# A graph kernel in which ScalarE casts the parts of the gathered table, loads ahead are spread over tiles, a bias product is in bf16, and the last unit is short

## The reference

```
xn = layernorm(x)
x  = x + gcn(xn, src, dst) + mix(xn)            # 256 -> 64, normalised sum over edges, -> 256; linear attention and MLP
h  = layernorm(x)
w  = softmax(h @ Wr + br)                       # 8 gates for each node
x  = x + sum over 8 experts of w[e] * (relu(bn(relu(bn(h @ W1[e])) @ W2[e])) @ Wo[e] + bo[e])
xn = layernorm(x)
x  = x + gat(xn, edges) + mix2(xn)              # graph attention, 8 heads; linear attention
x  = x + sum over 4 experts of g[e] * (gelu(x @ W1[e] + b1[e]) @ W2[e] + b2[e])
         # g: top-2 gates from a second graph attention with 4 heads x 4 experts, layernorm, softmax
```

## Time and profile before

| | us |
|---|---|
| median of 3 runs | 4652.31 (4649.49 to 4652.64) |
| profiled execution, its own time | 4653.68 |
| its span, first to last instruction | 4652.0 |
| TensorE busy | 3793.3 (82%) |
| GpSimd busy | 2800.2 (60%) |
| VectorE busy | 3181.6 (68%) |
| ScalarE busy | 2251.8 (48%) |

### The profile page before, as it was taken

The page is one execution under the profiler, slowest core; times in us unless marked ns, Lnnn a source line. Parts: engine busy times, 40 slices in busy tenths (PEclk is TensorE's granted clock), DMA queues, the critical chain, the costliest instruction groups (busy, mean ns, idle before and its releaser), DMA issues. The chain is left out here.

```text
span 4652.0 us, 67767 instructions
## 1 busy us (share of the span) xinstructions
PE 3793.3 (82%) x17826; PEld 2401.8 (52%) x17828; DVE 3181.6 (68%) x9935; ACT 2251.8 (48%) x4069; POOL 2800.2 (60%) x2880
## 2 busy tenths in 40 slices
PE   6797989999999999758888888887178887787776
PEld 6644556666666566534444444446144454444444
DVE  7775565454646455678888888886566777777776
ACT  7242223322322333357776765444366666666665
POOL 0174576565756410077777777773777777777774
PEclk9998999999999999888988988995588889988988
DMA  3233121111211100455555555653322222222221
GB/s 98 71 91 108 29 48 40 32 42 30 44 28 39 25 12 0 122 135 140 141 133 133 134 131 147 163 150 80 78 35 40 45 40 40 40 39 39 40 40 27
DMA packets 291562, 331.24 MB, mean 71 GB/s; under 512 B 80094, under 2 KB 245886, under 8 KB 291190
## 3 DMA queue, kind: packets, MB, share of 16 engines
q0 software_dynamic: 105328, 175.77, 18.5%
q1 hardware_dynamic: 185862, 151.14, 11.9%
HBM read 289.47 MB, written 30.77 MB: 69 GB/s over the span
## 5 line engine op out<-in xcount | busy, mean ns | idle before, releaser
L3035 POOL DMA_INDIRECT st_rows<-tabr,router_rsrc x1072 | 1022.8, 954 | 329.9 <-issue 321.5
L2388 POOL DMA_INDIRECT all_XT<-tab,graph_gsrc x880 | 855.1, 972 | 308.6 <-issue 244.7
L1416 POOL DMA_INDIRECT st_rows<-tab,graph_gsrc x748 | 742.0, 992 | 482.9 <-PE st_pe L1439 281.0
L1669 ACT ACTIVATE st_h<-st_ph,st_shift,st_scale 128x448 f32<-128x448 f32 x448 | 324.4, 724 | 753.4 <-PE st_ph L1527 753.3
L2418 PE MATMUL st_po<-all_XT,st_hot 128*128 128x264 f32 x1760 | 567.8, 459 | 37.6 <-DVE gat_sum L2609 36.4
L2609 DVE TENSOR_TENSOR gat_sum<-gat_sum,st_po 128x264 f32 x880 | 376.4, 428 | 145.1 <-DVE gat_sum L2609 98.5
L3080 PE MATMUL st_px<-all_XT,st_w 128*128 128x512 f32 (+1 forms) x832 | 423.2, 658 | 10.8 <-ACT st_hid L3140 10.8
L1756 DVE TENSOR_TENSOR gcn_acc<-gcn_acc,st_pe 128x65 f32 x748 | 166.4, 222 | 379.7 <-PE st_pe L1439 289.4
L2418 PEld LDWEIGHTS st_po<-all_XT,st_hot 128*128 128x128 f32 x1760 | 320.3, 211 | 198.7 <-DVE gat_sum L2609 122.5
L3092 PE MATMUL st_py<-st_w,st_hid 128*128 128x256 f32 x1568 | 420.0, 414 | 0.5 <-ACT st_hid L3140 0.5
L3053 PE MATMUL st_pad<-st_adr,st_hott 128*128 x1072 | 121.9, 183 | 345.6 <-DVE st_zd L3206 330.8
(11 more groups left out here) (507 smaller groups left out, 7221.5 us busy)
## 6 DMA issues: line engine op xcount, KB each, us to landing
st_bc<-drowr SPq DMA_DIRECT2D x268, 128.0 KB
st_bc<-drow SPq DMA_DIRECT2D x220, 128.0 KB
st_rows<-tabr,router_rsrc POOLq DMA_INDIRECT x1072
all_XT<-tab,graph_gsrc POOLq DMA_INDIRECT x880
st_xtb<-xtd SPq DMA_DIRECT2D x98, 128.0 KB
st_rows<-tab,graph_gsrc POOLq DMA_INDIRECT x748
tab<-gat_sum SPq DMA_DIRECT2D x7, 924.0 KB
xtd<-all_XT SPq DMA_DIRECT2D x49, 128.0 KB, 1.7
```

Source lines behind the costliest of these rows:

```text
L1416: g.indirect_dma_start(self.rows[:, b, u, :], None, self.R.tab0, bass.IndirectOffsetOnAxis(self.R.gsrc[:, t:t + 1], 0)).then_inc(self.s_ro ...
L1669: a.activation((self.h1, self.h2)[l][:, fb, h * HALF:(h + 1) * HALF], self.ph[:, m % 3, 0:HALF], ACT.Relu, bias=self.shift[:, l, i:i + 1], ...
L2388: g.indirect_dma_start(self.rows[:, b, u, :], None, self.R.tab1, bass.IndirectOffsetOnAxis(self.R.gsrc[:, t:t + 1], 0)).then_inc(self.s_ro ...
L3035: g.indirect_dma_start(self.rows[:, b, u, :], None, self.R.tabr, bass.IndirectOffsetOnAxis(self.R.rsrc[:, t:t + 1], 0)).then_inc(self.s_ro ...
```

## The change

There are four edits. In Front's end ScalarE does the two casts of each chunk, VectorE keeps the scaling and two subtractions, and a loop has three chunks under way: scaled(i), the first subtraction of i-1, the second of i-2. The wait for a free store buffer goes with the first cast to ScalarE.

In Prelude the load of registers moves ahead of the first tile, and the loads ahead are issued one behind each tile's load from tile 3 on. There are 24 of them, since `bo` is now loaded twelve times, into 96 partitions.

In Stage 1 the gates are split into three bf16 parts by seven more small instructions of VectorE in each chunk, and laid out over 96 rows, so that one bf16 product of 96 rows holds all products of parts that are kept. `bo` is split once, at the start of the stage.

In Stage 3 the units are eleven of four windows, one of three and one of two, each judged by itself. An update waits only for the last update of the same window.

```
-        self.bo = f.sb("bo", [E0, D])
+        self.bo = f.sb("bo", [PARTS * 32, D])
+        self.bop = f.sb("bop", [PARTS * 32, D], BF16)
...
+        _, ws = self.nc.values_load_multi_w_load_instructions(
+            self.R.gperm[0:1, 0:TPI], engines=(ENG.SP,), min_val=0, max_val=W - 1,
+            skip_runtime_bounds_check_because="a number of a window")
         for n in range(W):
...
-            if n == W // 2:
-                for to, of in loads:
-                    s.dma_start(to, of).then_inc(self.s_ahead, 16)
-                _, ws = self.nc.values_load_multi_w_load_instructions(
-                    self.R.gperm[0:1, 0:TPI], engines=(ENG.SP,), min_val=0, max_val=W - 1,
-                    skip_runtime_bounds_check_because="a number of a window")
-                for j in range(TPI):
-                    s.dma_start(self.R.ahead.xm[:, :, j * P:(j + 1) * P],
-                                self.R.xtd[bass.ds(ws[j], 1), :, :].rearrange("a p (c t) -> p (a c) t", c=C))\
-                        .then_inc(self.s_ahead, 16)
+            k = n - self.XTB
+            if 0 <= k < len(loads):
+                s.dma_start(*loads[k]).then_inc(self.s_ahead, 16)
+            elif 0 <= k - len(loads) < TPI:
+                j = k - len(loads)
+                s.dma_start(self.R.ahead.xm[:, :, j * P:(j + 1) * P],
+                            self.R.xtd[bass.ds(ws[j], 1), :, :].rearrange("a p (c t) -> p (a c) t", c=C))\
+                    .then_inc(self.s_ahead, 16)
...
+        def cast(i, k):
+            if 0 <= i < ITER:
+                x = self.xw[:, TPI * i:TPI * (i + 1), :]
+                if k == 0:
+                    a.wait_ge(self.s_scaled, i + 1)
+                    if i >= self.TABS:
+                        a.wait_ge(self.s_out[i % self.TABS], 16 * (i // self.TABS))
+                else:
+                    a.wait_ge(self.s_less, i + 1)
+                a.activation(self.tabt[:, i % self.TABS, :, k * GCOL:k * GCOL + GCN], x, ACT.Copy)\
+                    .then_inc(self.s_cast[k], 1)
+        for i in range(ITER + 1):
+            cast(i, 0)
+            cast(i - 1, 1)
...
-        def rows_cut(i):
...
-        for i in range(ITER):
-            rows_cut(i)
+        for i in range(ITER + 2):
+            scaled(i)
+            cut(i - 1, 0)
+            cut(i - 2, 1)
             put(i + 2)
...
-                mm = t.transpose(self.side[0:E0, (j - 4 * k) * P:(j - 4 * k + 1) * P], self.gate[:, n % 2, j, :],
+                mm = t.transpose(self.side[0:PARTS * 32, (j - 4 * k) * P:(j - 4 * k + 1) * P], self.gs[:, j, :],
...
-                mm = t.matmul(self.side[:, (j - 2 * k) * D:(j - 2 * k + 1) * D], self.gt[:, j, :], self.bo[:, :],
+                mm = t.matmul(self.side[:, (j - 2 * k) * D:(j - 2 * k + 1) * D], self.gt[:, j, :], self.bop[:, :],
...
+            if n:
+                v.wait_ge(self.s_side, self.at["gt", n - 1, 1] + 1)
+            st.then(v.tensor_copy(self.gb[:, :, :], self.gate[:, n % 2]))
+            st.then(v.tensor_copy(g4[:, :, :, 0:E0], every(self.gb[:, :, :])))
+            st.then(v.tensor_tensor(self.lg[:, :, :], self.gate[:, n % 2], self.gb[:, :, :], ALU.subtract))
+            st.then(v.tensor_copy(self.gb[:, :, :], self.lg[:, :, :]))
+            st.then(v.tensor_copy(g4[:, :, :, E0:2 * E0], every(self.gb[:, :, :])))
+            st.then(v.tensor_tensor(self.lg[:, :, :], self.lg[:, :, :], self.gb[:, :, :], ALU.subtract))
+            st.then(v.tensor_copy(g4[:, :, :, 2 * E0:3 * E0], every(self.lg[:, :, :])))
...
+        st.then(v.memset(self.gs[:, :, :], 0.0))
+        st.then(v.tensor_copy(self.bop[:, :], self.bo[:, :]))
+        for k in range(1, PARTS):
+            st.then(v.tensor_tensor(self.bo[:, :], self.bo[:, :], self.bop[:, :], ALU.subtract))
+            for b in range(k, PARTS):
+                st.then(v.tensor_copy(self.bop[32 * b:32 * (b + 1), :], self.bo[32 * b:32 * (b + 1), :]))
...
-        self.units = [(r, min(U, W - r)) for r in range(0, W, U)]
+        self.units = [(r, U) for r in range(0, last, U)] + [(last, W - self.LAST - last), (W - self.LAST, self.LAST)]
-        self.judged = [(r, U) for r in range(0, last, U)] + [(last, W - last)]
+        self.judged = list(self.units)
...
-            if self.moved:
-                v.wait_ge(self.s_x, self.moved)
+            if r in self.touched:
+                v.wait_ge(self.s_x, self.touched[r])
```

More of the change, by code:

```diff
@@ L241, in loads @@
                 (self.bg[:, :], spread(A.gcn_b)), (self.wr[:, :, :], rows(A.f0_wr)), (self.br[:, :], spread(A.f0_br)),
-                (self.bo[:, :], A.f0_bo), (self.bn[:, :, :, :], A.f0_bn))
+                (self.bn[:, :, :, :], A.f0_bn)) + tuple(
+                    (self.bo[E0 * k:E0 * (k + 1), :], A.f0_bo) for k in range(PARTS * 32 // E0))
 class Prelude:
@@ L329, in sync @@
         A = self.A
+        loads = self.R.ahead.loads(A)
+        assert self.XTB + len(loads) + TPI <= W
+        _, ws = self.nc.values_load_multi_w_load_instructions(
+            self.R.gperm[0:1, 0:TPI], engines=(ENG.SP,), min_val=0, max_val=W - 1,
+            skip_runtime_bounds_check_because="a number of a window")
         for n in range(W):
@@ L612, in __init__ @@
         self.s_xd = [f.sem(f"xd{j}") for j in range(self.SETS * TPI)]
+        self.s_scaled, self.s_less = f.sem("scaled"), f.sem("less")
+        self.s_cast = [f.sem(f"cast{k}") for k in range(2)]
         (self.s_made, self.s_keyed, self.s_columns, self.s_moved, self.s_ordered, self.s_tabbed, self.s_split, self.s_turned,
@@ L907, in put, with scaled, cut @@
             v.tensor_copy(R.gdst[:, j * P:(j + 1) * P], self.pt[:, j % 2, P:2 * P]).then_inc(self.s_put, 1)
-        def rows_cut(i):
-            part = [self.tabt[:, i % self.TABS, :, k * GCOL:k * GCOL + GCN] for k in range(PARTS)]
-            x = self.xw[:, TPI * i:TPI * (i + 1), :]
-            if i >= self.TABS:
-                v.wait_ge(self.s_out[i % self.TABS], 16 * (i // self.TABS))
-            norm = R.nsrc[:, TPI * i:TPI * (i + 1)].unsqueeze(2).to_broadcast([P, TPI, GCN])
-            st.then(v.tensor_tensor(x, x, norm, ALU.mult))
-            st.then(v.tensor_copy(part[0], x))
-            st.then(v.tensor_tensor(x, x, part[0], ALU.subtract))
-            st.then(v.tensor_copy(part[1], x))
-            v.tensor_tensor(part[2], x, part[1], ALU.subtract).then_inc(self.s_tab, 1)
+        def scaled(i):
+            if i < ITER:
+                x = self.xw[:, TPI * i:TPI * (i + 1), :]
+                norm = R.nsrc[:, TPI * i:TPI * (i + 1)].unsqueeze(2).to_broadcast([P, TPI, GCN])
+                v.tensor_tensor(x, x, norm, ALU.mult).then_inc(self.s_scaled, 1)
+        def cut(i, k):
+            if 0 <= i < ITER:
+                x = self.xw[:, TPI * i:TPI * (i + 1), :]
+                part = [self.tabt[:, i % self.TABS, :, m * GCOL:m * GCOL + GCN] for m in range(PARTS)]
+                v.wait_ge(self.s_cast[k], i + 1)
+                if k == 0:
+                    v.tensor_tensor(x, x, part[0], ALU.subtract).then_inc(self.s_less, 1)
+                else:
+                    v.tensor_tensor(part[2], x, part[1], ALU.subtract).then_inc(self.s_tab, 1)
         v.memset(R.X[:, W - 1, :], 0.0).then_inc(self.s_cleared, 1)
@@ L1307, in __init__ @@
         self.br = R.ahead.br
-        self.bo = R.ahead.bo
+        self.bo, self.bop = R.ahead.bo, R.ahead.bop
+        self.gs = f.sb("gs", [P, TPI, PARTS * 32])
+        self.gb = f.sb("gb", [P, TPI, E0], BF16)
         self.bn = R.ahead.bn
@@ L1329, in __init__ @@
         self.gate = f.sb("gate", [P, 2, TPI, E0])
-        self.gt = f.sb("gt", [E0, TPI, P])
+        self.gt = f.sb("gt", [PARTS * 32, TPI, P], BF16)
         self.h1 = f.sb("h1", [P, C, TOK])
@@ L2884 @@
     UNIT = 4
+    LAST = 2
     START = 23
@@ L2915, in __init__ @@
         U = self.UNIT
-        V = W - (W // U - 1) * U
+        V = U
         self.g20 = f.sb("g20", [P, V, FROW])
@@ L3187, in vector @@
         st = Steps(v, self.s_st)
-        self.moved = 0
+        self.moved, self.touched = 0, {}
         def one_hot(q):
@@ L3424, in finished @@
             s.wait_ge(self.s_x, self.final[u])
-            if r + n < W:
-                ws = self.ranked(ENG.SP, r, n, W - 2)
-                for j in range(n):
-                    s.dma_start(whole[:, bass.ds(ws[j], 1), :], R.X[:, bass.ds(ws[j], 1), :]).then_inc(self.s_out, 16)
-            else:
+            full = min(n, W - 1 - r)
+            ws = self.ranked(ENG.SP, r, full, W - 2)
+            for j in range(full):
+                s.dma_start(whole[:, bass.ds(ws[j], 1), :], R.X[:, bass.ds(ws[j], 1), :]).then_inc(self.s_out, 16)
+            if full < n:
                 s.dma_start(self.out[(W - 1) * P:N, :], R.X[0:N - (W - 1) * P, W - 1, :]).then_inc(self.s_out, 16)
```

9 lines of the change are left out of this document (6 added, 3 removed).

## The result

| | before | changed |
|---|---|---|
| median of 20 runs, us | 4649.08 | 4641.88 |
| ratio | | 0.9982, 95% interval 0.9976 to 0.9988 |
| profiled execution, us | 4653.68 | 4629.89 |

The change is 0.18% faster, about 8 us, where I forecast 27 us and a range of 4615 to 4640: faster, but by a third of it and outside the range. Three single runs far off (4746 and 5008 us of the changed kernel, 4830 us of before) are left out of the ratio. The profiled execution of before, 4653.68 us, lies 4.6 us over its median, and that of the changed kernel is one of the fastest of the changed kernel's runs, which lie between 4628 and 4649 us; before's lie closer, from 4642 to 4656 us. So the two traces show 24 us, and three later traces of nearly the same program have spans that are 15 to 26 us longer. That difference is the first thing to explain.

A forecast was written before the change was run, and what follows sets the result against it. The bound changes with the stage: TensorE in Stage 1, no engine in Stage 3's last loops. Terms -4.1 - 6.7 - 12.4 - 3.8 = -27.0 us from 4653.68 gave 4626.7, so 4626 for the median; range of 8 in 10: 4615 to 4640.

The forecast's parts named there:

- Stage 3: End of Stage 3: shorter last judging and eight updates, less partly covered work moved into the loops, -3.8 us.
- Front, up to the first instruction of the next phase: Front's end: with casts on ScalarE the last subtraction ends at 206.9 instead of 211.01, -4.1 us.
- load of registers at the head of Prelude: Prelude's head: the load, now ahead of the first tile's transfer, is fully on the path, 1.1 us more.
- Prelude's wait and slow tile: Prelude: the burst of loads costs one tile 4.9 + 2.9 = 7.8 us, which spreading the loads saves.
- Stage 1, the product at an equal clock: Stage 1: bf16 bias product saves 0.74 us a pair; of 18.5 us, waits leave -12.4.
- The sum's step to 204.2 us: Front's end: chunk 6's first cast waits for a free store buffer until about 204.2, at 1.4 us per further store.
- My lower end, -1: Front's end: the term's small end, -1 us, if stores take the 6.4 us of the slowest.
- The absorbing waits: Stage 1: TensorE's waits for the third (1.1 us) and fourth (2.5 to 3.0 us) bias additions take back some saving.
- an earlier product only waits longer: Stage 1: L1449 waits for VectorE's third bias addition in six chunks, so a shorter product there gains nothing.
- a rival in Prelude: Prelude: second transfers make 24 tiles late, TensorE runs at its lower level, 70 us lost, 4702 us; chance 0.03.
- the cover in the last loops: Last loops of Stage 3: VectorE's idle time covers 7.2 us of moved judging and updates; last judging begins 4.8 us later.
- Rival 2: End of Stage 3 no faster or slower: moved judging and table loads delay the last loops' products, +3.4, 4633 us; chance 0.2.

The follow-up runs named there:

- e1: The changed kernel once more, as it is, for a second trace: 4643.37 us, ratio 0.9988 to the kernel before.
- e2: The changed kernel with each update again waiting for the update before it: 4645.35 us, ratio 0.9989 to the kernel before.
- e4: The changed kernel with each update waiting for the one before, except in the last unit: 4642.05 us, ratio 0.9986 to the kernel before.
- e14: The kernel of e12 with Front's end as in the kernel before (VectorE casts): 4627.58 us, ratio 0.9958 to the kernel before.
- e13: The kernel before with the new units' products (3 and 2 windows), the last five windows still judged together: 4655.72 us, ratio 1.0021.
- e3: The kernel before with only the updates' waits relaxed: 4653.67 us, ratio 1.0008.
- e12: Changed kernel, Stage 3 as before but last twenty updates free of each other, each chunk's third and fourth bias products done three times: 4626.84 us, 0.9955.
- e16: The kernel of e12, with TensorE also turning the identity 14 times before waiting for the next chunk's rows: 4619.80 us, ratio 0.9944.

## Why the prediction was wrong, by its own steps

The largest miss is Stage 3, 13.1 us between forecast and measured; Front has 4.0 and Stage 1, both rows together, 2.9. The sum with what the traces measured, in us; the last column is the changed kernel's first trace and e1, e2 and e4 in the mean, against the first trace of before (in Stage 1 against the mean of the four with its product). The medians differ by 7.2 us:

| term | forecast | measured |
|---|---|---|
| Front, up to the first instruction of the next phase | -4.1 | -0.1 |
| load of registers at the head of Prelude | +1.1 | +1.2 |
| Prelude's wait and slow tile | -7.8 | -7.9 |
| Stage 1, the product at an equal clock | -12.4 | -17.0 |
| Stage 1, more time at the lower clock | 0 | +7.5 |
| Stage 3 | -3.8 | +9.3 |
| the stretches between | 0 | -1.0 |
| sum | -27.0 | -8.0 |

- **Front.** The step that failed is the end of the term: I took the last subtraction's 4.1 us as the phase's. It came (3.2 us), but the phase ends with the landing of the last store, and I had used landings only for when a buffer comes free. The last store is issued 2.2 to 3.2 us sooner in the four traces, and SP then waits longer for it, 5.3 to 6.4 us where it was 3.1. The sum's step to 204.2 us also has 1.2 us for "the smaller transfer ahead" for which it shows no row. My lower end, -1, was near the value, and e14 shows no more.
- **Registers' load and Prelude**: right in mechanism and size by the traces (first product of a tile to the last: 176.4 us in the mean, before 184.3). No timed run shows it by itself. With the load at its head SP issues the first tile's transfer 1.09 us behind VectorE's first instruction, where it was 0.09 us ahead (216.68 - 215.59, 216.48 - 216.57). The load is a whole 1.2 us on the path, though its first use comes only at tile 27, with the loads of chunk 0; no run has it elsewhere.
- **Stage 1.** The absorbing waits were named rightly, and took 7.2 us. But a pair takes 0.22 us and not 0.31, so that all products together save 7 x (3 x 0.83 + 0.52) = 21.1 us, and TensorE's waits on the edge sums became 2.7 us shorter: 21.1 - 7.2 + 2.7 = 16.6 us. The term at an equal clock was mis-sized by 4.6 us. The step that failed is "an earlier product only waits longer", priced at nothing. A longer wait had a price of its own, the lower clock behind it. The lower clock took back 7.5 us in the mean of these traces, of which a part came behind waits that didn't grow, and that part is unexplained. I had it only as a rival in Prelude, where it didn't come.
- **Stage 3.** The end behind the last judging was right: eight updates in 0.48 + 7 x 0.40 us, the judging even shorter. The step that failed is the cover in the last loops. I priced the moved judging and updates (that cost was 2.3 us), and took the products' plan as unchanged. The split of the products costs 8.2 us (e13), and TensorE's waits between halves that are joined through ScalarE's queue are 5.8 us longer there. Rival 2 had the place and the sign, with another mechanism and a bound of +3.4 that was too small.
- **Free updates** were priced by their pitch alone. That they hold up the gathers for 7 us stood in no term; it cost nothing more in the changed kernel, where the gathers were no longer the bound. In the kernel before they gave no gain either: e3 is at 4 us more (interval from none to 8).
- **Table loads.** By the Trainium skill (ScalarE: Activation LUTs, "What ACT_TABLE_LOAD costs") a switch takes 2.66 us. e13's rows show 1.28 us and the next activation 0.01 us behind it, so here the shorter price holds.
- **The updates' pitch.** By the Trainium skill (VectorE: DVE Perf Modes, "The DRAIN you can't avoid") a row without semaphores is no faster, which would have kept it at 0.53 us. In the changed kernel sixteen take 6.42 us, 0.40 each, so the measurement decides against it.

Of the base, 3.2 us were off too: the sum starts from a median of three runs, 4652.31 us, and that of twenty is 4649.08.

Still open: why Stage 1's clock falls so unevenly from run to run, and how much of each step of e12 and e16 is the clock's.

## What to carry to other kernels

A saving ahead of a wait is not simply worth nothing; in the traces it made the lower clock come more often. So look at the granted clock behind each wait of TensorE that an edit makes longer, and if it falls there, try to fill the wait or leave the product long. Where a phase ends on landings, read the last store's landing, and not the engine that feeds it. When a table of sizes feeds a planner, compare what it puts side by side in the last loops, for here two steps joined through another engine's queue cost more than all the instructions moved. Take several traces before believing a gain: here one execution showed 24 us, and the median 8.

## What the runs showed of the hardware

- An indirect gather's issue on GpSimd, 0.94 us, took up to 3.79 us while VectorE ran sixteen operations of two SBUF inputs and no waits between (6.42 us). In rows of eight and fewer none took over 1.3 us. With a wait between them, 0.13 us each, no gather took over 1.2 us (e2).
- Without waits the same operation took 0.477 us rather than 0.485, and its pitch was 0.40 us rather than 0.53.
- The same program spent 51.2 us of one stage at the lower clock in one execution and 88.7 in another, with the same waits.
- The clock fell to 1.2 GHz behind a wait of TensorE of 1.12 us in 4 of 24 cases, behind the same wait at 1.96 us in 22 of 36, and at 1.52 us in none of 24.
